# A transformer block in FFN, linear attention and expert zones: one order for all of it, and the score maxima as a second matmul

## What is computed

```python
def L0_attn(x):                                 # 16 heads of 8 channels, S = 1024
    Q, K, V = (x @ w + b for w, b in ((wq, bq), (wk, bk), (wv, bv)))
    Q, K, V = (a.reshape(B * H, S, D) for a in (Q, K, V))
    attn = softmax(einsum('bqd,bkd->bqk', Q, K) / sqrt(D), axis=-1)
    ctx = einsum('bqk,bkd->bqd', attn, V).reshape(B, S, E)
    return layernorm(ctx @ wo + bo + x) * gamma + beta

def L0_ffn(x):                                  # 128 -> 512 -> 512 -> 512 -> 128
    h = silu(tlin(x, w1_w, w1_s)) * tlin(x, w2_w, w2_s)
    h = gelu(tlin(h, h1_w, h1_s)); h = gelu(tlin(h, h2_w, h2_s))
    return tlin(h, w3_w, w3_s)                  # ternary weights

def L1_attn(x):                                 # gated linear attention, 8 heads, T = 1024
    for t: h = h * exp(gt)[..., None] + kt[..., None] * vt[..., None, :]; ot = einsum(qt, h)
    return (o * rms(o) * g_norm_w * silu(g)) @ Wo

def L1_ffn(x):                                  # router: the 3 best of 8 zones for each sequence
    return x + sum(w[e] * (gelu(x @ Wa[e]) @ Wb[e]) for e in zones)
```

## Time and profile before

| | |
|---|---|
| three runs | 1122.34, 1131.49, 1132.95 us; median 1131.49 |
| profiled execution | 1121.4 us, span 1119.5 us |
| granted TensorE clock, mean | 0.969 |
| last exponential of the attention | at about 540 us |
| busy share of the span | PE 91%, ACT 72%, DVE 58%, POOL 34% |
| DMA | 66.90 MB, 28% of 16 engines' time |

### The profile page before, as it was taken

One profiled execution on the slowest core, in us unless ns is written; L12 is line 12 of the kernel. 1 busy time (PEld: TensorE's weight loads), 2 busy tenths in 40 slices (PEclk: granted clock), 3 DMA queues, 4 the chain that ended last, 5 costly groups with the idle time before them and its releaser, 6 DMA issues.

```text
span 1119.5 us, 16637 instructions
## 1 busy us (share of the span) xinstructions
PE 1019.4 (91%) x5970; PEld 509.1 (45%) x5970; DVE 646.0 (58%) x1173; ACT 810.6 (72%) x1097; POOL 375.2 (34%) x317
## 2 busy tenths in 40 slices
PE   2799999999999999999698988888788899999998
PEld 1232333333333333333276655565355536666667
DVE  3121454526344443313464999999999899995200
ACT  2699999999999999999557667565656675455441
POOL 1000010101000010100153787798679767655100
PEclk7799999999999999999899999999799999999999
DMA  5766453625455452710101101100000122011200
GB/s 126 121 113 118 92 117 63 125 60 110 77 104 96 86 106 52 121 36 15 34 1 38 38 1 39 38 1 29 28 20 1 57 57 85 1 48 29 57 29 20
DMA packets 98780, 66.90 MB, mean 60 GB/s; under 512 B 61636, under 2 KB 84964, under 8 KB 96612
## 3 DMA queue, kind: packets, MB, share of 16 engines
q1 hardware_dynamic: 98656, 65.33, 28.0%
q10 hardware_dynamic: 24, 0.25, 0.1%
HBM read 46.41 MB, written 18.87 MB: 58 GB/s over the span
## 4 chain that ended last, share of the span: by engine, by line
PE 63%; DVE 19%; POOL 5%; issue 5%; ACT 3%; SPq 1%; DMA 1%; ACTq 0%; DVEq 0%; POOLq 0%
PE PS L1481 26%; PE PS L1466 15%; DVE R L1293 8%; PE PS L1652 6%; PE PS L1515 4%; DVE R L1284 4%; POOL R L869 3%; PE PS L1641 3%; PE PS L1555 2%; PE PS L1410 2%; DVE RB L1246 1%; DVE R L1252 1%; PE PS L1579 1%; PE PS L1396 1%; DVE R L1256 1%
## 5 line engine op out<-in xcount | busy, mean ns | idle before, releaser
L922 ACT ACTIVATE R<-PS 128x1024 f32<-128x1024 f32 x512 | 474.4, 1085 | 58.4 <-PE PS L1466 57.6
L1481 PE MATMUL PS<-R 128*32 128x512 f32 x2048 | 314.1, 607 | 1.2 <-issue 1.2
L869 POOL TENSOR_TENSOR R<-R 128x512 f32<-128x512 f32 x128 | 216.1, 1705 | 50.0 <-DVE R L1293 27.1
L1293 DVE TENSOR_TENSOR_SCAN R<-R 128x512 f32<-128x512 f32 x128 | 208.6, 1630 | 0.0
L1466 PE MATMUL PS<-RA 34*128 34x512 f32 x1024 | 189.2, 447 | 20.1 <-DMA RA<-QD 19.5
L1515 PE MATMUL PS<-RB,WR 128*128 128x512 f32 x640 | 174.8, 417 | 18.4 <-DVE R L1252 12.1
L1466 PEld LDWEIGHTS PS<-RA 34*128 34x128 f32 x1024 | 77.1, 186 | 216.2 <-issue 193.5
L1515 PEld LDWEIGHTS PS<-RB,WR 128*128 128x128 f32 x640 | 122.9, 195 | 63.0 <-DVE R L1252 14.3
L1481 PEld LDWEIGHTS PS<-R 128*32 128x32 f32 x2048 | 68.0, 108 | 106.1 <-issue 94.1
L855 POOL TENSOR_TENSOR RB<-R,RB 128x512 fp32r<-128x512 f32 x48 | 75.6, 1576 | 76.6 <-ACT RB L932 68.1
L845 POOL PARTITION_ALL_REDUCE R<-R x8 | 3.0, 376 | 287.6 <-DVE R L1133 287.6
(11 more groups left out here) (129 smaller groups left out, 1005.1 us busy)
## 6 DMA issues: line engine op xcount, KB each, us to landing
RA<-QD SPq DMA_DIRECT2D x256, 64.0 KB
QD<-RA SPq DMA_DIRECT2D x128, 64.0 KB, 2.1
RA<-QD SPq DMA_DIRECT2D x64, 128.0 KB
OD<-R SPq DMA_DIRECT2D x128, 32.0 KB, 2.0
R<-OD SPq DMA_DIRECT2D x128, 32.0 KB
VD<-RC SPq DMA_DIRECT2D x16, 256.0 KB, 2.3
RC<-VD SPq DMA_DIRECT2D x16, 256.0 KB
WP<-in_Wa SPq DMA_DIRECT2D x12, 256.0 KB, 3.2
```

The costliest lines, as they stand in the source:

```text
L869: pool.tensor_tensor(st, st, Qc[b % 2], ALU.mult).then_inc(S["qh"], 1)
L922: act.activation(PR[u % 4], bank(2 * s, 1024), ACT.Exp, scale=SC).then_inc(S["exp"], 1)
L1293: dve.tensor_tensor_scan(st, Ac[k], st, CS[:, v:v + 1] if k else 0.0, ALU.mult, ALU.add).then_inc(S["scanned"], 1)
L1481: op = pe.matmul(bank(ob)[c:c + 32, :], VAF[b % 2][:, at:at + 32], PR[u % 4][:, 512 * h:512 * h + 512], start=(j == 0), stop=(j == 7), til ...
```

## The change

Constants: `ST` has 6 buffers (was 10), `KQ` 3 (was 6), `OS` 1 (was 2); the zones keep 13 hidden tiles in a ring.

1. **One order.** `ORDER` now covers the whole program after the first block's preparation: x is a half step of attention (scores, then weighing of the pair before), f fetch, l load_pair, q the preparation of a block, a its closing, w the FFN's weights, b the FFN (one stream now), p, s, t, z, d as before, r the replicas. FFN, linear attention and output of finished blocks stand between the rounds of later blocks. The zones come after the last round.
2. **Banks.** From round 6 (`LATE`) on the units have two slots in banks 0 to 3, the context has bank 4, all other steps share 5 and 6, and 7 gathers.
3. **Scores.** A unit uses 32 rows instead of 34 (K first part against both parts of Q), a pair lies in four row groups; the maxima come as a second matmul with 8 rows (`GSEL`, `GQ`) into the same bank. `load_pair` is now 4 DMAs of keys and 8 of queries.
4. **Replicas** are DMAs from DRAM (`VD`) into `ST`; the product reads `ST` instead of PSUM.
5. **FFN parts**: VectorE makes all first parts; ScalarE's copies and second gelus go. ScalarE uses one table set for exp and log.

```diff
@@ load_pair (SP) @@
-                if n >= 6:
-                    need.wait_ge("scores", 16 * (n - 5))
-                for p in (0, 64):
-                    for r0, r1, i in KEY_PARTS:
-                        sp.dma_start(words(KS[k][p + r0:p + r1, :, :]),
-                                     bass.AP(QD.tensor, QD[1, b, i4, i, 0, 0:1].offset,
-                                             [[2048, r1 - r0], [1, 2048]])).then_inc(S["pair_in%d" % k], 16)
...
-                        sp.dma_start(words(QS[k][p + r:p + r + 16, :, :]),
-                                     bass.AP(QD.tensor, QD[0, b, i4, 0, 0, 8 * p:8 * p + 1].offset,
-                                             [[2048, 16], [1024, 2], [1, 512]])).then_inc(S["pair_in%d" % k], 16)
+                if n >= 3:
+                    need.wait_ge("scores", 16 * (n - 2))
+                keys(n, k, "pair_in%d" % k)
...
+                queries(n, k, "pair_in%d" % k)
+            def keys(n, k, landed):
+                for h in range(2):
+                    for gg in range(2):
+                        p = 32 * (2 * h + gg)
+                        sp.dma_start(words(KS[k][p:p + 32, :]),
+                                     bass.AP(QD.tensor, QD[1, n // 4, n % 4, 0, 0, 1024 * gg:1024 * gg + 1].offset,
+                                             [[0, 2], [2048, 16], [1, 1024]])).then_inc(S[landed], 16)
+            def queries(n, k, landed):
+                for h in range(2):
+                    for gg in range(2):
+                        for i in range(2):
+                            p, at = 32 * (2 * h + gg) + 16 * i, 1024 * gg + 512 * h
+                            sp.dma_start(words(QS[k][p:p + 16, :]),
+                                         bass.AP(QD.tensor, QD[0, n // 4, n % 4, i, 0, at:at + 1].offset,
+                                                 [[0, 2], [2048, 8], [1, 512]])).then_inc(S[landed], 16)
@@ scores (PE) @@
-                for h in range(2):
-                    p = 64 * h
-                    op = pe.matmul(bank(2 * s + h), exact(KS[k][p:p + 34, gg, 128 * j:128 * j + 128]),
-                                   exact(QS[k][p:p + 34, gg, :]), start=True, stop=True)
-                op.then_inc(S["scores"], 1)
+                slots = [(unit(u + gg)[5], gg) for gg in range(2)]
+                for s, gg in slots:
+                    for h in range(2):
+                        room(2 * s + h)
+                    for h in range(2):
+                        p = 32 * (2 * h + gg)
+                        pe.matmul(bank(2 * s + h), exact(KS[k][p:p + 32, 128 * j:128 * j + 128]),
+                                  exact(QS[k][p:p + 32, :]), start=True, stop=False)
+                for s, gg in slots:
+                    for h in range(2):
+                        p = 32 * (2 * h + gg)
+                        op = pe.matmul(bank(2 * s + h), view(GSEL[p:p + 8, n:n + 1], (0, 128)), exact(GQ[p:p + 8, :]),
+                                       start=False, stop=True)
+                        emptied[2 * s + h] = ("exp", u + gg + 1)
+                    op.then_inc(S["scores"], 1)
@@ replica: PE before, SP after; product (DVE) @@
-                pe.matmul(bank(bk), SPREAD[v % 8 // 4][:, v % 4, :], partC(RV[b % 2][:, v // 8, :]), start=True,
-                          stop=True).then_inc(S["replica_ps"], 1)
+                need.wait_ge("v_out", 16 * (b + 1))
+                if n >= NS:
+                    need.wait_ge("gather_ps", (n - NS) // 4 + 1)
+                if n >= 3:
+                    need.wait_ge("kv", n - 2)
+                sp.dma_start(ST[n % NS], bass.AP(VD.tensor, VD[b, 0, v, 0:1].offset,
+                                                 [[8192, 8], [0, 16], [1, 512]])).then_inc(S["rep_in%d" % (n % 3)], 16)
-                dve.tensor_tensor(ST[n % NS], bank(3 + v % 2), Kc[b % 2], ALU.mult).then_inc(S["kv"], 1)
+                need.wait_ge("rep_in%d" % (n % 3), 16 * (n // 3 + 1))
+                dve.tensor_tensor(ST[n % NS], ST[n % NS], Kc, ALU.mult).then_inc(S["kv"], 1)
@@ Plan @@
+    def take(self, who):
+        if self.acc < LATE:
+            return 6 + (self.acc + 1) % 2
+        banks = ((5, 6) if self.acc < 32 else
+                 {"b": (0, 1, 2), "d": (0, 1, 2), "o": (3, 4), "a": (4,), "c": (5, 6)}[who])
@@ ORDER, first line @@
-    "abcbbccbbccbbbacccbbbbbbbbacbbbbcacbcbcccbcapcbbcpbppbcpcppbpcpbcppbpppssssssbcssbcbscssssppsbssssbp"
+    "qqqxwqxxwxxxxwwxxxxxxxxxxxxxwlxxxxxxxxxxxxxwxxxqxxwxxxwxxxxfwxlxxfwxxxxwxxxxlxwxqxwxxxxwlxxxxxfxxxxx"
```

More of the change, by code:

```diff
@@ L82, in __init__ @@
         self.order, self.total = [], {}
[L83 to L87, removed]
+        self.done = {}
+        self.acc, self.turn, self.loaded = 0, {}, 2
+        self.weighed, self.closed = False, 0
         self.parts_of = {}
-        self.xt3, self.x3, self.xn = {}, {}, {}
-        self.attention()
+        self.xt3 = {}
+        self.start()
         self.rest()
@@ L98, in count @@
         return (name, self.total[name])
[L100 to L113, removed]
-        return e
@@ L177, in attention, with stats, apply, stats_shift @@
-    def attention(self):
-        self.stats("X", 0, 0, ("x_in0", 16))
+    def stats(self, k, where, b, *after):
+        n = self.count("bn_aggr_" + k)[1]
+        self.add("stats", k, where, b, n, self.done.get(k), after)
+        return n
+    def apply(self, k, to, where, b, n, *after):
+        e = self.done[k] = self.count("norm_" + k)
+        self.add("apply", k, to, where, b, n, e, after)
+        return e
+    def stats_shift(self, k, where, b, *after):
+        n = self.stats(k, where, b, *after)
+        self.add("shift", k, n)
+        return n
@@ new lines, in scale @@
+    def scale(self, k, to, where, b, n, *after):
+        e = self.done[k] = self.count("norm_" + k)
+        self.add("scale", k, to, where, b, n, e, after)
+        return e
+    def take(self, who):
[3 more added lines that the diff above has]
+                 {"b": (0, 1, 2), "d": (0, 1, 2), "o": (3, 4), "a": (4,), "c": (5, 6)}[who])
+        at = self.turn[banks] = self.turn.get(banks, -1) + 1
+        return banks[at % len(banks)]
@@ L179, in attention, with start @@
+    def norm_in(self, b):
+        n = self.stats("q", "X", b, ("x_in%d" % b, 16))
+        after = [("y_sum", b - 1)] if b >= 2 else []
+        return self.apply("q", "XN", "X", b, n, *after)
+    def start(self):
+        e = self.norm_in(0)
         self.add("pads", 0)
-        self.norm_in(0)
-        self.add("turn_in", 0, 1, self.xn[0])
+        self.add("turn_in", 0, 1, e)
         self.add("split", 0, 1, 2)
@@ L229, in attention @@
                     self.add("finish", pr - 1)
-                if w == 2 and pr:
-                    self.add("fetch", pr - 1)
-                for step in plan.get(8 * q + w, []):
-                    step(6 + (pr + 1) % 2)
+                    self.acc = pr
+                yield
         self.add("weigh", 510)
@@ L278, in level @@
             self.parts_of[key] = [None] * 2
[L279 removed]
+            bk = self.take("b")
             done = self.count("hid_ps")
             hi = self.count("gelu")
+            if n0 == 6:
+                self.parts_of[key][0] = hi
             self.add("hid_mm", n0, b, m, [("hl", src, k) for k in range(4)],
[L283 removed]
+                     [list(self.parts_of[earlier, b, k]) for k in range(4)], bk, hi)
```

986 lines of the change are left out of this document (462 added, 524 removed).

## The result

The changed kernel takes **1445.5 us** (median of 4 runs, 1440.3 to 1448.0) against 1127.5 us: a ratio of 1.281, 95% interval 1.273 to 1.290. Its profiled execution spans 1438.5 us. The prediction said 1390, slower with 0.93, and the number lies in its range. They do not act by the path that the sum assumed, and two errors of opposite sign brought the sum near the measured time. The kernels of the experiments were run two to four times each; times are medians.

The account below looks back on a forecast made before the run. Two DMA engines carrying the key and query loads bound the rounds: 1057 us on them from 24.7, rounds ending at 1109, plus 251 after the last exponential and 30 of queueing, 1390 us; range 1200 to 1530.

Parts of the forecast that it names:

- That two engines carry the loads: Attention's key and query loads: outermost source extent 2 lets only two of 16 DMA engines work; chance 0.80.
- Their speed: Rate of the two DMA engines: 17 GB/s each, 34 together, so 23.1 us for a round's 786 kB.
- The other traffic: Keeps, stores and fetches in the attention rounds: 73 engine-us per round, or 4.5 us on each DMA engine.
- The sum on the two engines: Loads, other traffic and replicas through the last round: 739 + 144 + 174 = 1057 us on the two DMA engines.
- The queueing behind the loads: VectorE's product waits for replicas issued behind loads: 0 to 138 us added, 30 taken.
- Signs that held: Expected in the profile: DMA share some 0.2, rounds 27 to 29 then 34 to 38 us, lower clock, 240 to 270 us tail.
- The 251 us of the end: After the last exponential: TensorE's remaining zone, FFN, gather and small matmuls, 251 us that nothing before can hide.
- Rival B: Attention rounds: loads spread over the engines and ScalarE binds, 1148 us in all; chance 0.10.
- 82 + 57: ScalarE's idle time in the rounds: 82 us from two score slots, 57 from gelu waits and longer TensorE insertions.
- Rival C: Attention rounds: loads spread and the order fills ScalarE's bubbles, so not slower, 1049 us; chance 0.04.
- D: Two engines bind at the low rate, 30.2 us per round, each replica queues behind a whole load: about 1680 us; chance 0.06.
- 88 x 1.30 = 114 us: ScalarE: table loads rise from 48 to 136, adding 114 us, said to hide under the loads.

Follow-up runs that it names:

- the last experiment: Rounds alone with one number changed (LATE 6 to 32), so the score banks serve as three slots in all 32 rounds: 1494.3 us, ratio 1.325.
- rounds alone: Changed kernel with wide loads; FFN, linear attention and zone steps moved from between the rounds to after the last round: 1572.2 us, ratio 1.401.

## Why the prediction was right, point by point

**That two engines carry the loads**: shown. (They were 8 and 16 before; the 32 in the prediction is an error that changes nothing.) The share is 0.13 where they flow alone, in two kernels; widening them gives 181 us back, narrowing them in the kernel before costs 196. The rule of the Trainium skill, page "DMA: Bandwidth & Descriptors", section "Why a DMA increments its semaphore by 16 and not by 1", agrees with that 0.13 for an outermost extent of 2.

**Their speed**: wrong. I carried 17 GB/s from rows with 8 and 15 busy engines down to two; the two moved 51 GB/s, so 25.5 each, and a round takes 15.4 us, not 23.1.

**The other traffic**, 4.5 us per round and engine: too much. In the narrowed kernel before, a round inside the rounds' stretch is 400 / 308 x 16 = 20.8 us; a share of 0.23 makes 76 engine-us of it, the loads 2 x 15.4 = 31, so 45 or 2.8 per engine. The wide loads of the earlier trace rows thus took some 119 - 45 = 74 engine-us, 10.6 GB/s each, if the other traffic takes the same time in both. The trace's packet records of that stretch give 12 GB/s for the keys' packets of 8 KB and 13 for those of 2 KB, so 74 is somewhat high; either way I had split the 119 the wrong way round.

**The sum on the two engines**, 1057 us: this step failed. It lets the two engines be full and set every round. With the measured values it is 32 x (15.4 + 2.8) + 174 = 756, far under the 1135 us that the rounds took. The engines weren't full: from 41 to 1175 us there was no packet in flight at all for 26% of the time. The sign I had named for it, over 200 us of score matmuls waiting for RA<-QD, came out at 43.7.

**The queueing behind the loads**: this was the path, and I had put it at 30 us in a range of 0 to 138. Going from wide to narrow, the replicas' wait alone rose by 114 us, those for weights and fetches by 22 and 30, and the time by 181. I had counted only a transfer's time behind the loads on the DMA engines, and had a stretch of SyncE's issues at nothing; SyncE's issuing grew from 16 to 24% of the span on the chain that ended last. And I had reasoned that a VectorE with slack absorbs the rest; but every engine walks one order, and at 438 us TensorE's FFN product stood 19.4 us behind the late cast.

**Signs that held**: share 0.20 (said: some 0.2); the later rounds 867.5 / 23 = 37.7 us (34 to 38). The first nine, 267.3 / 9 = 29.7, lie just above the 27 to 29, and only their mean is near: by the starts of the exponentials they take 15.7 to 54.1 us each. The clock fell to 0.83; 263 us after the last exponential with TensorE at 96% (240 to 270, over 90%). The 251 us of the end were 12 short.

**Rival B's 1148**, the price with wide loads: measured 1264.6. ScalarE's work in the rounds was near (723 said, 747 found); its idle time was 213 us, against 82 + 57. Two slots cost 78 us in the last experiment; that in mixed rounds most of the idle time is waiting for steps of other streams is not shown by a run of its own. Rival C's 1049 falls with it, and D's 1680 with its low rate: 13 GB/s against 25.5. The term "88 x 1.30 = 114 us" of table loads was right as busy time and nearly worthless as time: 26 us for 135 loads, more than the 88.

So the direction and the loads as main cause were right, and the closeness of 1390 was luck: the loads' price was too high (1390 - 1148 = 242, measured 181) and everything else too low (1148, measured 1265). 1445 - 1390 is the difference of the two errors, 117 - 61.

**What stays open**: the 88 us that remain when loads, table switches and maxima are taken out. They stand beside a granted clock of 0.91 in the rounds of that run (0.99 before) and rounds that wait for other streams; no run parts the two, and since the order was undone only crudely, none shows what the new pieces would give in the order of the kernel before. That the order also gives 308 us back against rounds alone is measured.

## What to carry to other kernels

Look at the outermost extent of every DMA pattern before its bytes: a repeat count of 2 put first turned 12 loads into two-engine loads, and another walk over the same bytes cost nothing. Such a transfer is not priced by its own landing but by what stands behind it: in the issuing engine's queue first, where a wait of 28.9 us had 21 us, and then until it has landed. So ask which store, fetch or weight load is issued after it, and who waits for that. And an engine's busy time taken out of a program whose engines walk one common order comes back only in small part: 172 us of ScalarE gave 26.

## What the runs showed of the hardware

A DMA engine's speed is not one number: 25.5 GB/s with two at work (0.13, 51 GB/s), against 16.6 with 8.3 and 17.6 with 15.2 at work. The shapes differ, but the size of a packet does not explain it: by the trace's records a packet of 2 KB takes 119 ns in the window with 8.3 at work and 85 to 87 ns in those with two.

SyncE's issues can stretch: the eight query loads of a round took 10.99 us to issue where with wide loads they took 5.97, and the line's median is 1039 ns against 655. It is not the shape of the load alone: with the keys wide and these same query loads narrow the median is 594 ns and the longest 713. The stretch comes with 786 KB a round on two engines and not with 262, which fits a backlog there, though no run shows what an issue waits for. In all, SyncE issued for 716 us in the changed kernel and for 579 with wide loads. The two rows are of the changed kernel and of the one with wide loads; min/median/max ns stand behind the count.

```profile
L707 SPq DMA_DIRECT2D RA<-QD x256: 593/1039/2904, 23.5 to 1104.6; - x128
```
```profile
L707 SPq DMA_DIRECT2D RA<-QD x256: 654/655/1393, 23.9 to 930.6; - x128
```
